# A decoder layer on one core: new instruction order in the first batch of attention, alternating query banks, routing counts in the prologue, and a ones product for two sums

## What is computed

```
x = x + attention(layernorm(x))    # 16 query heads of 128, one shared key and value head
x = x + experts(layernorm(x))      # each token's id picks one of 4 experts (512 x 512)
x = x + bitffn(layernorm(x))       # 512 -> 2048 -> 512, ternary weights, 8-bit activations
# attention, per batch:
xn = layernorm(x) * g_norm
q, k = l2norm(xn @ Wq) * 4, l2norm(xn @ Wk) * 4 ;  v = xn @ Wv
out = softmax(q k^T) v ;  attention = layernorm(out @ Wout) * g_out
# ternary weights: w -> clip(round(w * s), -1, 1) / s,  s = 1 / mean(|w|), over the whole matrix
```

## Time and profile before

| quantity | value |
|---|---|
| median of 3 runs | 1084.36 us (1082.53 to 1085.66) |
| time of the profiled execution | 1088.8 us |
| its span, first to last instruction | 1087.1 us |
| mean granted clock of PE | 0.956 of full |
| busy: PE, DVE, ACT, POOL | 935.1, 743.1, 546.5, 206.0 us |
| DMA, mean rate | 121 GB/s, engines 53% busy |

### The profile page before, as it was taken

The page is one execution under the profiler, slowest core; times in us unless marked ns, Lnnn a source line. Parts: engine busy times, 40 slices in busy tenths (PEclk is TensorE's granted clock), DMA queues, the critical chain, the costliest instruction groups (busy, mean ns, idle before and its releaser), DMA issues.

```text
span 1087.1 us, 18880 instructions
## 1 busy us (share of the span) xinstructions
PE 935.1 (86%) x6538; PEld 519.7 (48%) x6538; DVE 743.1 (68%) x1637; ACT 546.5 (50%) x1517; POOL 206.0 (19%) x337
## 2 busy tenths in 40 slices
PE   0687889889999998999999999998942899569996
PEld 0344546545656564565665655664411344224442
DVE  4248896666877575778576767784421399889894
ACT  2557766766675674676667676753110221123330
POOL 1212211102221223132222121211320021101111
PEclk9989999999999998999999999999966899969999
DMA  9315645355576353555434444479349852216564
GB/s 265 84 39 117 146 108 120 96 145 127 150 171 165 108 120 86 135 124 116 113 91 117 105 108 106 105 156 189 107 120 214 165 112 49 49 24 146 131 126 97
DMA packets 305662, 131.85 MB, mean 121 GB/s; under 512 B 275232, under 2 KB 279840, under 8 KB 305568
## 3 DMA queue, kind: packets, MB, share of 16 engines
q1 hardware_dynamic: 301728, 118.03, 48.7%
q0 software_dynamic: 3840, 12.60, 3.4%
HBM read 42.76 MB, written 20.99 MB: 59 GB/s over the span
## 4 chain that ended last, share of the span: by engine, by line
PE 60%; DVE 17%; SPq 7%; ACT 6%; issue 5%; DMA 3%; POOL 2%; DVEq 1%; ACTq 0%; POOLq 0%
PE S L236 5%; PE S L238 5%; PE S L237 5%; PE QB L236 5%; PE QB L237 4%; PE QB L238 4%; PE S L644 4%; PE OUTB L236 4%; PE OUTB L237 4%; PE OUTB L238 4%; PE O L544 4%; PE O L542 4%; PE O L546 4%; SPq L430 3%; DVE P L1024 2%
## 5 line engine op out<-in xcount | busy, mean ns | idle before, releaser
L544 PE MATMUL O<-V,P 128*128 128x128 f16 x1024 | 179.2, 221 | 0.0
L542 PE MATMUL O<-V,P 128*128 128x129 f16 x1024 | 179.0, 219 | 0.0
L546 PE MATMUL O<-V,P 128*128 128x129 f16 x1024 | 178.9, 218 | 0.0
L1024 DVE TENSOR_TENSOR P<-P 128x1024 f16<-128x1024 f32 x128 | 156.8, 1225 | 4.4
L1012 DVE SCALAR_TENSOR_TENSOR QTOKR<-QB,rn,QTOKR 128x128 f16<-128x128 f32 x240 | 67.6, 344 | 119.6 <-ACT QTOKR L737 119.4
L756 ACT ACTIVATE OTOK<-O,rd 128x128 f16<-128x128 f32 x256 | 79.4, 365 | 132.9 <-DVE rd L1029 132.9
L745 ACT ACTIVATE P<-S,cst 128x1024 f32<-128x1024 f32 x128 | 140.0, 1130 | 12.0 <-PE S L238 11.5
L236 PE MATMUL QB<-WQA,XQA 128*128 128x512 f16 x240 | 93.5, 390 | 41.6 <-DVE QTOKR L1012 27.9
L1360 POOL TENSOR_SCALAR qst<-qs 128x4 f32<-128x4 f32 x64 | 18.2, 284 | 498.3 <-ACT junk L728 490.6
L544 PEld LDWEIGHTS O<-V,P 128*128 128x128 bf16 x1024 | 99.2, 97 | 7.4
L542 PEld LDWEIGHTS O<-V,P 128*128 128x128 bf16 x1024 | 98.4, 96 | 7.8 <-issue 0.3
(11 more groups left out here) (195 smaller groups left out, 1799.2 us busy)
## 6 DMA issues: line engine op xcount, KB each, us to landing
SIDE<-in_L_ffn_w_dram SPq DMA_DIRECT2D x64, 256.0 KB, 3.2
OTA<-sorted_rows SPq DMA_DIRECT2D x4, 1028.0 KB, 7.0
OTA<-in_L_attn_Wq_dram SPq DMA_DIRECT2D x4, 1024.0 KB, 11.6
SIDE<-in_L_attn_Wout_dram SPq DMA_DIRECT2D x16, 256.0 KB, 3.0
SIDE<-in_ctx_dram SPq DMA_DIRECT2D x16, 256.0 KB, 3.2
ctx_split<-SIDE SPq DMA_DIRECT2D x16, 256.0 KB, 2.7
ROWB<-in_x_dram SPq DMA_DIRECT2D x16, 256.0 KB, 3.3
w_tern<-SIDE SPq DMA_DIRECT2D x32, 128.0 KB, 2.9
```

What stands on the lines that cost most here:

```text
L542: nc.tensor.matmul(o, ph(g)[:, a:a + P], V[:, b % 2, j, 0:129], start=j == 0, stop=False)
L544: nc.tensor.matmul(o[:, 0:128], ph(g)[:, a:a + P], V[:, b % 2, j, 130:258], start=False, stop=False)
L546: last = nc.tensor.matmul(o, pl(g)[:, a:a + P], V[:, b % 2, j, 0:129], start=False, stop=j == NT - 1)
L1024: nc.vector.tensor_tensor(pl(g)[:, cols], P32[:, cols], ph(g)[:, cols], ALU.subtract).then_inc(p_lo, 1)
```

## The change

- **SP, start of the program:** of the four quarters of `Wq` only the first is loaded ahead of the transposes of the input; the second follows them and the last two come after the first query tiles. The token ids are loaded before `Wq`. `g_out` (a broadcast load) moves to step 4. In a step, `turn_q(g+4)` now stands behind the loads of inputs, rows and context.
- **PE:** the two small products of the routing counts come first of all, ahead of `keys_values(0)`, and wait for `routing_counts`. Only four query tiles are made ahead of step 0; `queries(4)` follows `scores(0)`. In a step `outputs` precedes `queries`. Query tiles of odd number below 20 go to `OUTB`, so that `queries(u)` waits for tile `u-2`. From tile 20 on, only `QB` is used. `keys_values` now writes `S`, bank 0, and `scores` of the next step waits for its copy.
- **ACT:** `query_squares(g+4)` comes ahead of the exponentials of step `g`, `query_high(g+4)` behind them.
- **DVE:** `query_low(g+4)` moves between the two halves of the probabilities. The routing moves to the prologue: counts and places behind the first quarter of `Wq`, pairs behind the second.
- **Weight sums:** none in steps 0 to 13, two a step in steps 14 to 29.
- **The two scales:** a product with an fp32 matrix of ones on PE in step 32 takes the place of POOL's all-reduce.
- **First outputs:** they wait for 4 heads of `Wout` at a time instead of all 16.

The core of the diff:

```diff
         def qbank(u):
-            return S[:, u * 512:(u + 1) * 512] if u < 4 else QB[:, :]
+            return S[:, u * 512:(u + 1) * 512] if u < 4 else OUTB[:, :] if u % 2 and u < 20 else QB[:, :]
 
         def kvbank(n):
-            return O[:, n * 512:(n + 1) * 512] if n < 2 else QB[:, :]
+            return O[:, n * 512:(n + 1) * 512] if n < 2 else S[:, 0:512]
...
         def piece_at(g):
-            return [p for p in range(2 * HEADS) if p - (p >= HEADS) == g]
+            return [p for p in range(2 * HEADS) if HEADS - 2 + p // 2 == g]
...
@@ queries(u), PE
-                if u >= 5:
-                    pe.wait_ge(q_lo, u)
-                for n in range(2, 8):
-                    if kv_at(u - AHEAD) == n:
-                        pe.wait_ge(kv_f, n + 1)
+                if 6 <= u < 20:
+                    pe.wait_ge(q_lo, u - 1)
+                elif u >= 20:
+                    pe.wait_ge(q_lo, u if u > 20 else 19)
@@ scores(g), PE
+                    if half == 0 and kv_at(g - 1) is not None:
+                        pe.wait_ge(kv_f, kv_at(g - 1) + 1)
@@ outputs(n), PE
                 if n == 0:
-                    pe.wait_ge(wo_lo, HEADS)
-                    pe.wait_ge(pos_ready, 2)
+                    pe.wait_ge(q_lo, 20)
+                if t == 0 and b == 0:
+                    pe.wait_ge(wo_lo, 4 * (q + 1))
...
@@ main list, PE
             pe.wait_ge(consts, 1)
+            pe.wait_ge(counts, 2)
+            nc.tensor.matmul(QB[:, 0:E * TILES], lower[:, :], scm[:, :], start=True, stop=True)
+            nc.tensor.matmul(QB[:, 64:64 + E * TILES], onesb[:, :], scm[:, :], start=True, stop=True
+                             ).then_inc(rank_ps, 1)
             keys_values(0)
             keys_values(1)
-            for u in range(AHEAD):
+            for u in range(NT):
                 queries(u)
             for g in range(STEPS):
                 scores(g)
+                if g == 0:
+                    pe.wait_ge(pos_ready, 1)
+                    queries(4)
+                if g == 2 * HEADS:
+                    pe.wait_ge(w_scale, 1)
+                    pe.wait_ge(out_cp, 4)
+                    nc.tensor.matmul(OUTB[:, 0:2], onesf[:, :], wsc[:, 0:2], start=True, stop=True
+                                     ).then_inc(w_total, 1)
                 if g >= 1:
                     values(g - 1)
                 if kv_at(g) is not None:
                     keys_values(kv_at(g))
+                if g >= HEADS:
+                    outputs(g - HEADS)
                 if g + AHEAD < STEPS:
                     queries(g + AHEAD)
-                if g >= HEADS:
-                    outputs(g - HEADS)
-                if g == 4:
-                    (the two products of the routing counts)
@@ main list, ACT
-                if g + 4 < STEPS:
-                    query_high(g + 4)
+                if g >= 1 and g + 4 < STEPS:
+                    query_squares(g + 4)
                 for half in range(2):
                     exponentials(g, half)
+                if g == 0:
+                    query_squares(4)
+                if g + 4 < STEPS:
+                    query_high(g + 4)
+                if g >= 1:
+                    head_high(g - 1)
                 if kv_at(g) is not None:
                     kv_copy(kv_at(g))
-                if g >= 1:
-                    head_high(g - 1)
-                if g + AHEAD < STEPS:
-                    query_squares(g + AHEAD)
@@ main list, DVE
-                if g + 4 < STEPS:
-                    query_low(g + 4)
                 probabilities(g, 0)
+                if g == 2 * HEADS:
+                    weight_scales_set()
                 if g >= 1:
                     head_sums(g - 1, 0)
+                if g + 4 < STEPS:
+                    query_low(g + 4)
                 probabilities(g, 1)
@@ main list, POOL
-                if g == 2 * HEADS - 1:
-                    pool.wait_ge(w_scale, 1)
-                    nc.gpsimd.partition_all_reduce(wsc[:, 2:4], wsc[:, 0:2], P, RADD).then_inc(w_total, 1)
```

More of the change, by code:

```diff
@@ L363, in _, with load_wq @@
             sp.dma_start(wkv_st, Wkv.rearrange("(c p) n -> p c n", p=P)).then_inc(wkv_in, 16)
[L364 removed]
+            def load_wq(q):
                 sp.dma_start(OTA[:, q * 2048:(q + 1) * 2048].rearrange("p (c n) -> p c n", c=DC),
@@ L369, in _ @@
                          allow_slow_non_contiguous=True).then_inc(ids_in, 16)
-            sp.dma_start(GO[:, :], g_out.partition_broadcast(P)).then_inc(go_in, 16)
+            load_wq(0)
+            for k in range(NT):
+                turn_x(k)
+            load_wq(1)
             for h in range(2):
                 load_wout(h)
-                load_sum(h)
-            for k in range(NT):
-                turn_x(k)
             turn_k(0)
@@ L378, in _ @@
                 turn_q(u)
+            for q in range(2, 4):
+                load_wq(q)
             for g in range(STEPS):
                 b, h = divmod(g, HEADS)
-                if g + 4 < STEPS:
-                    turn_q(g + 4)
                 if h == 14 and b + 1 < B:
```

54 lines of the change are left out of this document (24 added, 30 removed).

## The result

The changed kernel takes **1076.93 us** (median of 7 runs, 1072.77 to 1079.89). The kernel before, on the same chip, takes 1084.54 (7 runs, 1082.53 to 1087.69). The ratio is 0.9927, 95% interval [0.9905, 0.995]: faster by 0.5 to 1%. The forecast was 1051 with a range of 1038 to 1066, so the sign was right and the size was not: of 33.8 us that the sum promised, 7.6 came.

What follows compares the result with a forecast made beforehand. It took a ring over four engines to bound steps 0 to 16 and PE the steps from 17. Its terms, -33.8 us, took 1088.8 to 1055.0; 4.4 less for the median gave 1050.6, stated as 1051, range 1038 to 1066.

Steps and rivals of the forecast that it cites:

- Part 1, first product: Start of the program: PE's first product comes at 21.3 us in place of 28.65, -7.3 us.
- Part 2, first scores: Start of step 0: `scores(0)` goes ahead of `queries(4)`, at 46.8 us and at half clock, -6.35 us.
- Part 3, the ring: Steps 0 to 16: the loop of dependent work over four engines shortens to 8.36 or 10.13 us a step, -11.6 us.
- Now lies beside the exponentials: POOL's norm, 1.55 us, leaves the ring of the first batch; 0.2 a step allowed for its new place, +3 us.
- It fits with nothing to spare, in one step of four: First batch: `turn_q` landing (2.7) and half of `scores` (1.3) take 4.05 us, where ACT wants it 4.1 after.
- And 9.9 on, is `scores(17)`: End of the first batch: `scores(17)` starts 9.9 us after the second conversion of step 15.
- Part 4, steps 17 to 31: PE's 10.51 us a step narrowly covers ACT's ring with two weight sums; +1.5 us, bounds 0 and 6.
- Part 5, keys and values: Keys and values in bank `S`: four waits of 0.78 us of the queries behind step 17 go, -3.1 us.
- Part 6, the scales: Steps 32 to 33: PE's wait and the half clock behind it go, -6.9 us, bounds 4 and 6.9.
- Part 7, the rest: From step 33 to the end: PE stays the bound, and nothing is gained or lost.
- the first batch keeps its pace: Rival: POOL or `turn_q` ends last and a first-batch step stays near 10.4 us; 1063 us, chance 12%.
- The norm waits out one conversion: Rival: POOL's norm is shut out by one conversion, 1.35 us later a step; 1079 us, about no change, chance 4%.

Runs made afterwards that it cites:

- e5: The changed kernel with the edits of both e1 and e2: 1058.54 us.
- e1: The changed kernel with the next query tile's power put ahead of the two scale instructions of the step before in POOL's list: 1065.14 us.
- e2: The changed kernel with twelve more, overwritten products on PE in steps 4, 8 and 16, ahead of the wait for the turned query: 1069.18 us.
- e3: The changed kernel with the order inside a step put back as before on all five engines: 1063.59 us.
- e7: e3 with one bank for the queries of step 5 and later, each waiting for the low half of the one before: 1065.66 us.
- e8: e3 with twelve more, overwritten products on PE ahead of the wait for the turned query in steps 8 and 16: 1060.72 us.
- e12: e5 with the weight sums one a step in steps 0 to 30, in place of two a step in steps 14 to 29: 1063.62 us.
- e10: e7 with the next batch's keys and values in the query bank as before the change: 1070.66 us.
- e6: The kernel before the change with only the ones product in place of POOL's all-reduce: 1082.32 us, ratio 0.9965.
- e9: e5 with POOL's all-reduce after step 31 in place of the ones product: 1064.39 us, ratio 0.9816.
- e11: e5 with 32 more products into the free output bank between the first queries and the first scores: 1058.80 us.

## Why the prediction was wrong

**Part 1, first product: right.** 21.33 for 21.3. The ids ahead of `Wq` cost nothing that shows, the lower bound.

**Part 2, first scores: right.** 46.41 for 46.8, at half clock, 5.3 us for the twelve.

**Part 3, the ring: the step that failed.** The sum of 8.36, and of 10.13 where ACT waits for `input_norm`, was right to 0.02 us wherever nothing else came in: steps 9 to 10 and 10 to 11 of the changed kernel take 8.36 and 8.35, and step 7 takes 10.11. In e5 the second conversion of step 15 comes 156.8 after `scores(0)`, for 153.4 plus the 3 allowed. That total is partly luck: the 3 were for the norm, which costs nothing in steps 6, 10 and 11 of e5 (8.34 each), while step 8, a group start at half clock, takes 10.78 for 8.36. In the changed kernel the way from `scores(0)` to `scores(17)` took 176.69 for 166.3: 4.0 more came up to the second conversion of step 15 and 6.4 behind it (16.26 for 9.9). What failed is what stood around the sum of a step:

- *"Now lies beside the exponentials", the norm.* Only how fast POOL works beside DVE was costed, with 0.4 taken as the most that could come. Where the norm stands in POOL's list was not asked. Before, the norm of tile g+4 was made in step g-1, ahead of that step's `input_rstd` and `out_rstd`. The edit moved it to the head of step g, and so behind these two, which wait for nearly the last thing DVE does in a step. The prediction went through SP's list for just this fault and not through POOL's. Its price was 11.8 us (e1), 4.5 of it from `scores(0)` to `scores(17)`; the rest shows in parts 4 and 7.
- *"It fits with nothing to spare, in one step of four", the turn.* The landing of 2.7 was right. But in that step PE has nothing else to do, rests 3.4 to 5.0 us, and then does `scores` at half clock, which the sum of 4.05 against 4.1 left out. It had used that same effect one part earlier, for `scores(0)`. Its price was up to 7.7 us (e2), of which the trace shows 3.5 from `scores(0)` to `scores(17)`.
- *"And 9.9 on, is `scores(17)`."* This held for a step whose `scores` had already begun. Step 16 opens a group, so `scores(16)` itself waits for a transpose that is issued only as the second conversion of step 15 begins (203.89 in e5): 3.1, then a full step of PE of 10.52, 13.6 in all. e5 shows exactly that (203.78 to 217.38), and the changed kernel 16.3 with the half clock.
- *The gain was credited to the wrong part.* The -11.6 were put down to the turned order with its two banks. e3 has the old order and reaches `scores(17)` at 223.31, the changed kernel at 223.10; e7 has one bank as well, and reaches it at 223.51. Of the removed waits of PE for `query_low` (29.3 us) all but the one ahead of `queries(5)` had no price, and what that one gave (4.4 us in e3 against e7) went in good part at `scores(16)`, 2.8 of it. With both repairs the turned order is at best a little faster than the old one with its own: 1058.5 against 1060.7, with overlapping intervals.

**Part 4, steps 17 to 31: mis-sized.** +1.5 forecast; the stretch from step 17 to 33 took 179.18, and 173.69 in e3, e7, e8 and e12, so 5.5 were lost. Most of it was POOL's list once more, as e1 has 174.86. The doubled sums, which the prediction had named as the sign to watch, are the other 1.1 (174.79 in e5, 173.69 in e12); one a step costs 5 in the first batch.

**Part 5, keys and values: right in kind,** 3.75 behind step 17 (e10 against e7) for 3.1; with the two in the first batch 5.0 by the medians.

**Part 6, the scales: right in the trace,** 6.9 for 6.9; by the whole time 3.8 (e6) and 5.9 to 8.2 (e9).

**Part 7, the rest: 8.1 us off.** 4.5 of it by the last `scores` product (307.1 for the 302.6 that the keys' term left), where the low half was late again, for the same cause: e1 takes 303.8. The last 3.6 are within what kernels that differ only in attention show: that stretch takes from 349.8 us (e5) to 357.3 (e7) in the profiled executions.

**From 1055.0 to 1050.6: not borne out.** The sum took 4.4 us off because the profiled execution of before lay that far above its median. The changed kernel's lies at its median, and e5's at 1058.0 for a median of 1058.5. What made the profiled execution of before longer stays open; against the 1055.0 of the sum itself e5 is 3 us off.

Of the rivals, "the first batch keeps its pace" came nearest in kind: POOL or `turn_q` ends last and a step stays near 10.4. It was 10.39 from `scores(0)` to `scores(17)`, and both links cost time there. It gave 1063: what the same links cost behind step 17, 3.9 us to `scores(33)` and 4.5 from `scores(34)` on, was not in it. The signs that the prediction named for being wrong came too: ACT waits for the norm, `scores` for `XQA<-QTOKR`, and PE for the low half in steps 22, 23 and 26.

"The norm waits out one conversion" named the right link, POOL's norm, by the wrong mechanism: a slow instruction, not a queue. That is why it got 4% and the "0.4 is the most a row shows" against it. It gave 1079, and that 1077 was measured is luck. On that mechanism the trace is mixed. In the step shown above `qst` takes 0.92 in place of 0.20 and ends at 117.04, where DVE's pass over two SBUF operands ends at 116.99: POOL did wait that pass out. The Trainium skill (SBUF — State Buffer, Who interferes with whom) says that DVE with two SBUF inputs and a GpSimd read exclude each other for the whole instruction, and this row agrees. But it comes to 0.7 us here. A power takes 1.01 alone and 1.40 to 1.42 in 31 of the changed kernel's 64 rows, and only in three rows does it lose 1.0 us or more (2.60 at 72.34, 2.00 at 374.04, 1.99 at 416.28), each beside a conversion. e1 has the powers of 1.4 too and is 11.8 us faster. That "0.4 is the most a row shows" was misread: the kernel before has six powers of 1.51 to 1.56, the first at 81.18 beside DVE's passes over `Wq`.

## What to carry to other kernels

When an instruction moves to another place in a step, write down for every in-order queue what now stands ahead of it and what that waits for; do it for the small engine that is 20% busy as for the others. A wait that the profile puts first can be slack nearly everywhere: ask of each of its places what the engine would do next if it ended, and whether the ring around it gets shorter. One part of a change can hide another, as the clock at the group start hid the second bank here, so test the one with the other mended. Where a bound engine rests at a fixed place, price the rest and the slower clock behind it together.

## What the runs showed of the hardware

- PE's granted level after a rest differed at equal rests: after 2.36 us (e2, step 4) the products took 0.38 us, after 2.37 us (e5, step 4) 0.58 to 0.63, and after 0.97 (e11) and 1.47 us (e5, step 16) 0.38. After the rests of 3.4 to 5.0 us in the changed kernel the first of them took 0.58 or more each time. At step 8 of e5 (rest 2.37) the first three took 0.38 and the next ones 0.51 to 0.63: the level fell while PE was at work again.
- A TENSOR_SCALAR of POOL on a tile of 128x1 or 128x4 took 0.18 to 0.20 us at the least and up to 1.63 beside DVE's passes over `Wout` and over the probabilities (`rst`, at 72.70 in e1). A power of 128x4 took 1.01 at the least and 2.60 beside the passes over `Wq`, `Wout` and the probabilities (at 72.34 in the changed kernel).
- The two-column fp32 product with a ones matrix, with its weights, took PE 0.28 us and replaced an all-reduce on POOL. In e9 POOL rested 7.68 us right behind the all-reduce, with no releaser shown; in the kernel before a DMA issue of POOL stands between it and the rest of 7.70.
